# The opening of a fused attention and mixture-of-experts kernel on one core, written in another order

## The reference

```
xn  = layernorm(x)
q, k, v = xn @ Wq.T + bq, xn @ Wk.T + bk, xn @ Wv.T + bv      # 16 heads of 32
s   = q k^T / sqrt(32), causal, plus ALiBi bias (slope per head)
att = softmax(s) v, then @ Wo.T + bo
p   = softmax(xn @ gate_w.T); top 2 of 8 experts, weights made to sum to 1
ffn = sum over the two experts of w * (silu(g) * u) @ w2[e].T,  [g, u] = xn @ w1[e].T
out = x + att + ffn
```

## Time and profile before

| | |
|---|---|
| median of 3 runs | 1620.87 us (1618.1 to 1623.33) |
| the profiled execution: its time, its span | 1621.4 us, 1619.6 us |
| TensorE, VectorE, ScalarE, GpSimd busy | 91%, 64%, 55%, 35% of the span |
| granted TensorE clock, mean | 0.974 |
| HBM over the span | 91 GB/s |

### The profile page before, as it was taken

One profiled execution on the slowest core, in us unless ns is written; L12 is line 12 of the kernel. 1 busy time (PEld: TensorE's weight loads), 2 busy tenths in 40 slices (PEclk: granted clock), 3 DMA queues, 4 the chain that ended last, 5 costly groups with the idle time before them and its releaser, 6 DMA issues.

```text
span 1619.6 us, 35530 instructions
## 1 busy us (share of the span) xinstructions
PE 1471.8 (91%) x12763; PEld 894.1 (55%) x12763; DVE 1043.0 (64%) x2494; ACT 888.4 (55%) x2020; POOL 567.1 (35%) x595
## 2 busy tenths in 40 slices
PE   3799998998998999999899798999789999999995
PEld 1465565555555555555555466665356656556662
DVE  6688787675878777777888978777243333333331
ACT  4378676664777776776866465677212222222221
POOL 3111033121113222112311224131216777777775
PEclk9899999998999999999999999999999999999998
DMA  7243531433333254442314242235687888888884
GB/s 256 66 130 105 146 92 52 106 107 105 109 109 92 91 141 130 137 130 86 109 45 123 78 120 62 67 89 179 241 228 118 137 125 139 138 138 126 134 142 46
DMA packets 171350, 193.28 MB, mean 119 GB/s; under 512 B 87536, under 2 KB 121072, under 8 KB 171056
## 3 DMA queue, kind: packets, MB, share of 16 engines
q1 hardware_dynamic: 143760, 151.67, 34.8%
q0 software_dynamic: 26128, 37.24, 14.0%
q10 hardware_dynamic: 1296, 2.11, 0.3%
HBM read 93.45 MB, written 53.74 MB: 91 GB/s over the span
## 4 chain that ended last, share of the span: by engine, by line
PE 69%; DVE 11%; issue 6%; DMA 4%; ACT 4%; SPq 4%; POOL 2%; POOLq 0%; DVEq 0%; ACTq 0%
PE S L1187 16%; PE T L1110 11%; PE O L1126 7%; PE S L1067 5%; PE S L1099 5%; PE M L1067 5%; PE M L1218 4%; PE O L1218 4%; DVE arena L1492 4%; SPq L944 3%; PE M L1149 2%; PE S L1084 2%; PE M L1084 2%; DVE arena L1503 1%; PE T L1202 1%
## 5 line engine op out<-in xcount | busy, mean ns | idle before, releaser
L1492 DVE CUSTOM_DVE_ANT_0 arena<-S,cF,nsl 128x1024 f32<-128x1024 f32 (+7 forms) x512 | 413.1, 811 | 69.7 <-PE S L1099 47.3
L1682 ACT ACTIVATE arena<-arena,mneg 128x1024 f32<-128x1024 f32 (+7 forms) x512 | 395.3, 772 | 60.2 <-DVE mneg L1492 59.5
L1110 PE MATMUL T<-cF,arena 128*128 128x128 f32 x2304 | 366.7, 280 | 64.6 <-ACT arena L1696 35.9
L1696 ACT ACTIVATE arena<-T 128x512 f32<-128x512 f32 (+3 forms) x536 | 242.4, 466 | 252.1 <-PE T L1110 249.2
L1110 PEld LDWEIGHTS T<-cF,arena 128*128 128x128 f32 x2304 | 268.6, 143 | 166.2 <-issue 50.5
L1187 PE MATMUL S<-arena 128*128 x1704 | 269.1, 315 | 10.5 <-issue 10.5
L1835 POOL DMA_INDIRECT out<-arena x142 | 221.9, 1562 | 106.8 <-ACT arena L1742 60.4
L1187 PEld LDWEIGHTS S<-arena 128*128 128x128 f16 x1704 | 167.4, 98 | 109.1 <-issue 11.8
L1503 DVE COPY arena<-T 128x512 f32<-128x512 f32 (+3 forms) x296 | 151.7, 516 | 112.6 <-PE T L1110 111.2
L1126 PE MATMUL O<-arena 128*32 128x128 f32 (+1 forms) x3328 | 212.6, 331 | 7.4 <-DVE arena L1523 6.3
L1099 PE MATMUL S<-arena 96*128 96x512 f16 (+3 forms) x768 | 212.9, 332 | 3.3 <-DMA arena<-arena 1.7
(11 more groups left out here) (187 smaller groups left out, 1819.4 us busy)
## 6 DMA issues: line engine op xcount, KB each, us to landing
arena<-arena SPq DMA_DIRECT2D x192, 128.0 KB, 2.4
arena<-in_w1T SPq DMA_DIRECT2D x64, 352.0 KB, 3.4
arena<-in_x SPq DMA_DIRECT2D x64, 256.0 KB, 3.4
w_d<-arena SPq DMA_DIRECT2D x32, 352.0 KB, 2.9
arena<-w_d SPq DMA_DIRECT2D x16, 704.0 KB, 7.1
arena<-in_w2T SPq DMA_DIRECT2D x32, 256.0 KB, 2.9
out<-arena SPq DMA_DIRECT2D x32, 256.0 KB, 3.2
xn_d<-arena SPq DMA_DIRECT2D x24, 256.0 KB, 2.0
```

The lines of the kernel that those rows point to most:

```text
L1110: tp = pe.transpose(z[:, (c - c0) * P:(c - c0 + 1) * P], ring[u % 4][:, c * P:(c + 1) * P], idf)
L1492: dve.tensor_tensor_reduce(ring[r][:, 0:w], SBK[o.bank["score", u]][:, 0:w], rel[:, S - w:S], nsl[:, hh:hh + 1], 3.0e38, ALU.add, ALU.min, ...
L1682: act.activation(ring[r][:, 0:w], ring[r][:, 0:w], ACT.Exp, bias=mneg[:, m:m + 1], scale=-1.0, accum_out=rs[:, k, c:c + 1]).then_inc(sems[ ...
L1696: act.activation(PT[k][:, h, to_:to_ + gap * (c1 - c0 - 1) + 1:gap, :], TB[o.bank["tr", u, i]][:, 0:n].rearrange("p (c n) -> p c n", n=P), ...
```

## The change

- The second place's four `ln_tile` steps and four transpose turns move behind the weight maxima. All four `tops` come first; of the `ln_tile`s, two stand between `tops` and the first half of the fold (`gmax`, `gtop` of part 0), two before its second half; two of the turns stand before the first projected tile, two behind it.
- The turns of batch 0 use the two `T` banks instead of the `M` banks.
- `w_part`: piece 0 becomes three, q, k and v of the first group (4 x 128 = 512 columns each); the other four pieces become numbers 3 to 6. The first q, k and v tiles each wait for their own piece. Later groups wait for number 6.
- `scales 1` becomes three: 1 (what q's and k's copies need), 3 (the columns `cq`, `bq`, `bk`) and 4 (gate, slopes, ramp). 3 and 4 stand behind the first splits.
- Pieces 3 to 6 are split between the steps of the first group's projection.
- `otop` moves from the job `first_rest` to the end of that projection; `woh` and `wol` are done in two halves of 1024 columns.
- The first group's k tiles go through `raw` instead of `t32`, and the second place's halves stand in the region of `PT1` instead of `st`. What waited for the latter's transposes and stores at `qkh` waits at the turned tiles of units 8 and up, and the first two `wload`s wait for the k low half.

```diff
 def ln_turn(b, half, i):
-        take_m(*key)
+        bank = "M" if b else "T"
+        if b:
+            take_m(*key)
+        else:
+            o.take("T", *key)
...
-    for half in range(2):
-        for i in range(7):
-            if i > 2:
-                ln_turn(0, half, i - 3)
-                flush()
-            if i < 4:
-                ln_tile(0, half, i)
-        if half == 0:
-            add("tops", 0)
+    for i in range(7):
+        if i > 2:
+            ln_turn(0, 0, i - 3)
+            flush()
+        if i < 4:
+            ln_tile(0, 0, i)
     load["act"] = load["dve"]
-    for c in range(1, 4):
+    for c in range(4):
         add("tops", c)
...
     for part in range(2):
-        for _ in widest("w", part):
-            pass
+        first = widest("w", part)
+        next(first)
+        ln_tile(0, 1, 2 * part)
+        ln_tile(0, 1, 2 * part + 1)
+        next(first)
     add("scales", 0)
     add("wqh", 0)
+    add("scales", 1)
+    add("wqh", 1)
     add("wql", 0)
-    for c in range(4):
-        add("wqh", 1 + c)
-    add("scales", 1)
+    add("wql", 1)
+    add("scales", 3)
+    for i in range(2):
+        ln_turn(0, 1, i)
+        flush()
+    add("wqh", 2)
+    add("wqh", 3)
+    add("wql", 2)
+    add("scales", 4)
     start = qkv_steps(0, 0)
     for i in range(16):
         next(start)
         flush()
-        if i == 5:
-            add("wql", 1)
+        if i == 2:
+            for t in (2, 3):
+                ln_turn(0, 1, t)
+            flush()
+            add("wqh", 4)
+        elif i == 4:
+            add("wql", 3)
+        elif i == 6:
+            add("wqh", 5)
+        elif i == 8:
+            add("wql", 4)
+        elif i == 10:
+            add("wqh", 6)
+    next(start)
+    add("otop")
     for _ in start:
         flush()
-    for c in range(1, 4):
-        add("wql", 1 + c)
+    add("wql", 5)
+    flush()
+    add("wql", 6)
...
-        return w[:, :, :, 0:P] if part == 0 else w[:, part - 1, :, P:E]
+        return w[:, :, part, 0:P] if part < 3 else w[:, part - 3, :, P:E]
...
+    def t32_at(b, g, qk, half):
+
+        return raw[:, 1, 0:512] if b == g == 0 and qk else t32[:, 0, :]
...
-    XH = [xh[:, k, :] for k in range(3)] + [st[:, k, :] for k in range(4)]
+    XH = [xh[:, k, :] for k in range(3)]
+    XH += [arena[:, PT1_AT + 2048 + k * E:PT1_AT + 2048 + (k + 1) * E].bitcast(F16) for k in range(4)]
...
-                if (b, g, qk, half) != (0, 0, 0, 0):
-                    n = 4 * (b * NG + g) + 2 * half + qk - 1
-                    on.wait_ge(sems["qkl"], n + 1)
+                n = 4 * (b * NG + g) + 2 * half + qk
+                if n > 3:
+                    on.wait_ge(sems["qkl"], n)
+                elif n > 1:
+                    on.wait_ge(sems["qkl"], n - 1)
```

More of the change, by code:

```diff
@@ L195, in rest @@
             o.count["xt", b, half, i] = o.count["xt", b, half, i, en]
-            o.leave("M", key, ("xt", b, half, i))
+            o.leave(bank, key, ("xt", b, half, i))
         later.append(rest)
@@ L565, in first_rest @@
         yield
-        add("woh")
+        add("woh", 0)
         yield
-        add("wol")
+        add("wol", 0)
+        add("woh", 1)
+        yield
+        add("wol", 1)
         yield
@@ L964, in sync @@
                     on.wait_ge(*at(*o.emptied[step]))
+                else:
+                    on.wait_ge(*at("qkl", 0, 0, 1, 1))
                 src = T["w1T"][x][:, c, :] if c < 4 else T["w2T"][x, (c - 4) * P:(c - 4) * P + rows, :]
@@ L1018, in tensor @@
                     on.wait_ge(*at(*s))
-                tz = MBK[o.bank[step]][:, :].bitcast(F16)
+                tz = (MBK if key[0] else TB)[o.bank[step]][:, :].bitcast(F16)
                 k = half_place(*key)
@@ L1074, in tensor @@
                 if i == 0:
-                    on.wait_ge(*at("wql", 4 if b or g else 0))
+                    on.wait_ge(*at("wql", 6 if b or g else 2))
                     for t in range(4):
@@ L1468, in vector @@
                         on.wait_ge(*at("stack", gb, gg, h))
-                else:
-                    for t in range(3, 7):
-                        on.wait_ge(*at("xtp", 0, t // 4, t % 4))
-                        on.wait_ge(*at("xnd", 0, t // 4, t % 4))
-                dve.tensor_copy(st[:, 2 * qk, lo:hi], t32[:, 0, :]).then_inc(sems["qkh"], 1)
+                dve.tensor_copy(st[:, 2 * qk, lo:hi], t32_at(*key)).then_inc(sems["qkh"], 1)
             elif kind == "vsb":
@@ L1502, in vector @@
                     on.wait_ge(*at("pv", u // 8 * 8 - 9))
+                elif u >= 8:
+                    on.wait_ge(*at("wol", 1))
+                    for t in range(3, 7):
+                        on.wait_ge(*at("xtp", 0, t // 4, t % 4))
+                        on.wait_ge(*at("xnd", 0, t // 4, t % 4))
                 dve.tensor_copy(PT[k][:, h, to_:to_ + gap * (c1_ - c0_ - 1) + 1:gap, :],
@@ L1640, in scalar @@
                 tt = half * 4 + i
-                tz = MBK[o.bank["xtp", b, half, i]][:, :].bitcast(F16)
+                tz = (MBK if b else TB)[o.bank["xtp", b, half, i]][:, :].bitcast(F16)
                 on.wait_ge(*at("xtp", b, half, i))
@@ L1692, in scalar @@
                 else:
-                    on.wait_ge(*at("wql", 4))
+                    on.wait_ge(*at("wql", 6))
                     if u >= 8:
-                        on.wait_ge(*at("wol"))
+                        on.wait_ge(*at("wol", 1))
+                        for t in range(3, 7):
+                            on.wait_ge(*at("xtp", 0, t // 4, t % 4))
+                            on.wait_ge(*at("xnd", 0, t // 4, t % 4))
                 act.activation(PT[k][:, h, to_:to_ + gap * (c1 - c0 - 1) + 1:gap, :],
```

45 lines of the change are left out of this document (24 added, 21 removed).

## The result

The changed kernel takes **1608.62 us** median (1606.45 to 1613.05, 7 runs) against 1620.87 beside it (1613.85 to 1623.65, 7 runs): ratio 0.9925, 95% interval 0.9904 to 0.9945. A second measurement beside other kernels gave 1604.17 against 1617.61, ratio 0.9911 (0.9894 to 0.9927). The forecast was 1608. The profiled execution took 1608.96, with a span of 1607.2.

What follows compares the result with a forecast made beforehand. The opening, a chain over five engines, was taken to bound the kernel, its gain moving everything behind it forward. -11.7 - 1.5 - 0.3 + 0.3 = -13.2 from 1621.4 gave 1608.2, predicted as 1608 us, range 1602.5 to 1613.

Steps and rivals of the forecast that it cites:

- Step 1: Opening up to the first projected tile: fold at 23.05 us instead of 30.61, tile at 29.4 instead of 37.34, -7.9.
- the hold: VectorE's two-input steps wait for GpSimd's low halves before the first tile: 1.1 us for the split, 0.2 for a tiny step.
- the bound of 32: First projected tile at 32 us if all VectorE's small steps in the scale chain were held by GpSimd.
- Step 2: The four q and k tiles, first tile to stacking: 17.8 us, +1.3; stacking at 47.2 instead of 53.9.
- Step 3: Stacking to the first row maximum: VectorE is late, not the stack; 53.5 us against 60.75, -7.3.
- Step 4: Wo's maximum ahead of the first row maximum: TensorE's 5.9 us wait goes, third row maximum 55.6 against 67.35, -11.7.
- Step 5: Clock behind the first row maximum: if it holds, fifth row maximum at 59.0, otherwise 60.5; -1.5, other bound 0.
- Rival B: The clock falls in TensorE's new gaps, or GpSimd's hold costs up to 3 us: gain 9 to 12; chance 0.23.
- Step 6: Wo's split in halves: TensorE's wait for a turned tile's copy about 1.0 us shorter; -0.3, between 0 and -1.
- the 40 copies: 40 of 832 turned-tile copies change engine, four more to VectorE in all: +0.3, bounds 0 and 2.4.
- Rival C: The wait and cold stretch around 80 us vanish too: gain 14.5 to 18, 1603 to 1606.5; chance 0.14.

Runs made afterwards that it cites:

- e1: The changed kernel run again without an edit, against the kernel before; 1604.17 us, ratio 0.9911.
- e9: The changed kernel with GpSimd writing zeros instead of the second place's last two low halves; 1603.98 us, ratio 0.9913 to the kernel before.
- e6: The changed kernel with the first group's q and k tiles again through one fp32 buffer; 1606.11 us, ratio 0.9896 to the kernel before.
- e10: The changed kernel with the last two weight splits moved earlier, between projected tiles and between v writes; 1602.07 us, ratio 0.9903 to the kernel before.
- e2: The changed kernel with the maximum of Wo back behind the first row maximum; 1609.80 us, ratio 0.9955 to the kernel before.
- e7: The kernel before with only the maximum of Wo moved ahead of the last v step; 1618.30 us, ratio 0.9970 to the kernel before.
- e4: The changed kernel with the second place normalized and turned again ahead of three weight maxima and the fold; 1611.47 us, ratio 0.9960 to the kernel before.
- e8: The changed kernel with the 40 turned-tile copies that changed engine put back on their old engines; 1603.46 us, ratio 0.9900 to the kernel before.
- e5: The changed kernel with Wo's high and low halves again each done in one stretch; 1605.66 us, ratio 0.9896 to the kernel before.

## Why the prediction was right, point by point

**What bounds the kernel.** Right: the opening was a chain, and what it gained moved everything behind it forward. The 14 attention stretches show no systematic loss beyond their scatter.

**Step 1, fold and first tile: right, the hold sized too large.** The fold came at 22.36 (22.82 in e1) for 23.05, since the turn ahead of it ran at 21.53 and not at 21.98 as in the earlier trace rows. From fold to tile it took 5.85 for 6.35. The seven small steps ran at 0.19 spacing beside GpSimd, as taken; they were not held, so the bound of 32 was never near. The tiny two-input step took 0.28 for 0.16, the split 1.34 for 0.75. I had taken 1.1 + 0.2 for the hold; e9 puts 0.6 on it. By the Trainium skill ("SBUF — State Buffer", Who interferes with whom) a VectorE instruction with two SBUF inputs contends with a GpSimd instruction that reads SBUF, not with one that only writes it, and the one that comes second is blocked for the whole instruction of the other; e9 agrees with the classes, by 2.91 against 1.42. That the wait was not a whole GpSimd step of 1.15 may be because the step was already under way when the split came; this was not tried.

**Step 2, q and k tiles: mis-sized, too slow by 1.4 to 2.8.** I forecast 17.8 from tile to stack; it was 14.99 in the first trace and 16.44 in e1. Behind the first tile's end I had 12.5 and it was 11.34 in both. The term that failed is the two transpose turns, 1.03 each from the earlier trace rows. In that row their matmuls stand 0.11 us apart, and behind the first tile half of that, so both took 1.06 together:

```profile
31.69 1.06 PE L1059 MATMUL T<-idh,arena 128*128 128x128 f16 x16
```

The rest is the first tile itself, 3.64 and 5.10 for 5.30. Without k's buffer it costs 1.3 more (e6), and that is absorbed before M1.

**Step 3, first row maximum: right.** It is 6.04 from stack to M1 for 6.3, with VectorE late, as e10 shows by turning it round.

**Step 4, Wo: right.** M3 came 1.98 behind M1 in the first trace and 2.93 in e1, for 2.1; e2 brings back 6.60. Done alone it gives 4 to 5 us (e7), undone it costs 5.6 to 7.1 (e2). Forecast for Steps 4 and 5 together were 13.2 - 7.3 = 5.9.

**Step 5, the clock: the mechanism right, the size and the certainty not.** M1 to M5 is 5.2 us where the clock stays and 7.7 to 7.8 where it has fallen, with e6 (6.2) and e4 (6.6) between: up to 2.6 us for a fall, not 1.5. And it is not decided by the program: the changed kernel did both. Rival B's fall of the clock was thus there in some executions.

**Step 6 and the 40 copies: each mis-sized, together about nothing.** I booked -0.3 and +0.3. Up to U8 the copies cost 0.9 (e8). From M5 to U8 the changed kernel takes 30.60 us and the kernel before 30.67, so something else gave the 0.9 back. Rival C's condition came true: the long wait and the cold stretch around 80 us are gone, and from 72 to 100 the granted clock is 1.00 for 0.94. It brought nothing in the sum because the copies' new places took as much. The halves by themselves are worth nothing there (e5), since the copy that waited behind Wo's split had moved to VectorE. What the clock alone gave was not tried.

**The sum.** The forecast of -13.2 stands against -12.25 and -13.4 measured by the medians, 12.2 and 14.4 by the ratios. The main parts are the right ones, but the closeness is partly luck. Steps 1 and 2 were too dear by some 2 to 4 us. Against that I treated the clock behind M1 as held, and it fell wholly or in part in five of the eleven traces with Wo's maximum in its new place and the new opening. And attention's own scatter between executions, up to 12 us, is as large as the gain.

## What to carry to other kernels

In an opening, look for the step that waits in an engine's queue behind work it doesn't need: here the fold of the scale behind four turns (7 us) and a 2.3 us reduction behind the first row maximum (4 to 5 us); these were the two largest single parts. Before costing a buffer or a faster piece, ask which engine is late at the next meeting point: the 1.3 us of e6 vanished there, because they were the stack's and VectorE was late, while the 0.6 of e9 and the 1.2 of e10 arrived. Trace one program twice before reading a difference of a few us between two traces, and find the stretches whose length repeats: there a single trace told 0.6 and 0.9 us apart, which no timed median here could.
